# Moving the second modulation of an adaLN block from the rows to the turned expert tiles

## The reference

```python
mod = (silu(c) @ wmod).reshape(2, 6, 1, 128); sa, ca, ga, sb, cb, gb = mod
h = layernorm(x) * (1 + ca) + sa
x = x + ga * recurrence(h)            # block-diagonal gates, then y[t] = a[t]*y[t-1] + b[t]
h = layernorm(x) * (1 + cb) + sb      # the second modulation: by batch, by column
logits = silu(h @ rw1 + rb1) @ rw2 + rb2          # 128 -> 512 -> 8
top 2 of 8, softmax over the two
out = sum_e we * (silu(h @ w1[e] + b1[e]) @ w2[e] + b2[e])
x = x + gb * out
```

## Time and profile before

| | |
|---|---|
| three runs | 289.06, 290.06, 291.38 us; median 290.06 |
| the profiled execution | 288.09 us, its span 286.2 us, so 1.9 us lie outside the span |
| busy in the span | PE 248.1, DVE 188.4, POOL 171.6, ACT 166.5 us |
| mean granted TensorE clock | 0.956 |

### The profile page before, as it was taken

One profiled execution on the slowest core, in us unless ns is written; L12 is line 12 of the kernel. 1 busy time (PEld: TensorE's weight loads), 2 busy tenths in 40 slices (PEclk: granted clock), 3 DMA queues, 4 the chain that ended last, 5 costly groups with the idle time before them and its releaser, 6 DMA issues.

```text
span 286.2 us, 4950 instructions
## 1 busy us (share of the span) xinstructions
PE 248.1 (87%) x1179; PEld 178.0 (62%) x1179; DVE 188.4 (66%) x750; ACT 166.5 (58%) x322; POOL 171.6 (60%) x192
## 2 busy tenths in 40 slices
PE   7767759997599798999999999999999999989910
PEld 6424334444144245687878888888888888868700
DVE  3959999999999987576444444444444446866533
ACT  4189979999785355545555555555555556445300
POOL 4996211267777757777777777644554445645650
PEclk9997979999779799999999999999999999999995
DMA  7993011121131226413533333222217822280505
GB/s 222 308 333 117 19 40 38 37 75 50 55 121 48 89 82 157 114 47 115 149 84 85 111 101 109 57 75 75 74 46 214 221 72 74 84 256 4 161 0 147
DMA packets 45365, 30.51 MB, mean 107 GB/s; under 512 B 5085, under 2 KB 41999, under 8 KB 45342
## 3 DMA queue, kind: packets, MB, share of 16 engines
q1 hardware_dynamic: 40432, 21.75, 27.9%
q0 software_dynamic: 4544, 8.47, 9.0%
q10 hardware_dynamic: 366, 0.04, 0.1%
HBM read 16.39 MB, written 12.67 MB: 102 GB/s over the span
## 4 chain that ended last, share of the span: by engine, by line
PE 40%; POOL 27%; issue 14%; DVE 12%; DMA 4%; POOLq 1%; DVEq 0%; SPq 0%; ACT 0%
POOL sorted_rows L550 21%; PE bank L1218 18%; PE bank L1205 18%; POOL shared L514 3%; PE bank L1226 3%; PE bank L1194 2%; DVE st L698 2%; DMA expert_out<-shared,tx 2%; POOL rs L506 1%; DVE shared L718 1%; POOL expert_out L559 1%; DVE tx L792 1%; DMA xs<-in_L_attn_x_dram 1%; DVE xs L803 1%; DMA tx<-sorted_rows 1%
## 5 line engine op out<-in xcount | busy, mean ns | idle before, releaser
L559 POOL DMA_INDIRECT expert_out<-shared,tx x78 | 80.4, 1031 | 52.9 <-DVE shared L1012 37.4
L657 ACT ACTIVATE hT<-bank,w_t 128x256 f32<-128x256 f32 x156 | 65.4, 470 | 29.3 <-PE bank L1205 28.3
L550 POOL DMA_INDIRECT sorted_rows<-rows,sloti x64 | 63.9, 999 | 27.2 <-issue 18.3
L1205 PE MATMUL bank<-xT,w_t 128*128 128x256 f32 x312 | 74.1, 380 | 0.1
L1218 PE MATMUL bank<-hT,w_t 128*128 128x256 f32 x312 | 74.1, 380 | 0.0
L1205 PEld LDWEIGHTS bank<-xT,w_t 128*128 128x128 f32 x312 | 56.3, 190 | 6.8 <-DVE w_t L995 0.7
L1218 PEld LDWEIGHTS bank<-hT,w_t 128*128 128x128 f32 x312 | 56.2, 190 | 6.2
L666 ACT ACTIVATE yT<-bank,w_t 128x256 f32<-128x256 f32 x39 | 18.4, 473 | 47.6 <-PE bank L1218 47.6
L1134 PE MATMUL bank<-h2T,rw_s 128*128 128x512 f32 x64 | 36.8, 677 | 1.7 <-ACT qv L644 1.4
L986 DVE COPY xT<-bank 128x256 f32<-128x256 f32 x39 | 16.5, 422 | 23.6 <-PE bank L1194 23.6
L1012 DVE TENSOR_TENSOR shared<-bank,tx 128x256 f32<-128x256 f32 x39 | 16.5, 423 | 21.3 <-PE bank L1226 21.2
(11 more groups left out here) (194 smaller groups left out, 328.9 us busy)
## 6 DMA issues: line engine op xcount, KB each, us to landing
tx<-sorted_rows SPq DMA_DIRECT2D x39, 130.0 KB, 2.2
w_s<-in_L_ffn_w_dram SPq DMA_DIRECT2D x16, 256.0 KB, 6.1
xs<-in_L_attn_x_dram SPq DMA_DIRECT2D x8, 256.0 KB, 5.2
rows<-rows SPq DMA_DIRECT2D x8, 256.0 KB, 2.6
av<-expert_out SPq DMA_DIRECT2D x8, 256.0 KB, 3.7
qv<-expert_out SPq DMA_DIRECT2D x6, 256.0 KB, 5.0
expert_out<-shared,tx POOLq DMA_INDIRECT x78, 2.3
sorted_rows<-padr SPq DMA_DIRECT2D x9, 130.0 KB, 3.0
```

The source lines that it names most:

```text
L550: p.indirect_dma_start(sorted_rows[:, :], bass.IndirectOffsetOnAxis(ap=sloti[:, k, t:t + 1], axis=0), rows[:, t, k, :], None).then_inc(s_d ...
L559: p.indirect_dma_start(expert_out[:, :], bass.IndirectOffsetOnAxis(ap=xr_i[:, s % U, n, D + 1:D + 2], axis=0), yo[:, s % U, n, :], None, b ...
L657: ins = nc.scalar.activation(hsT[:, u % 2, h, :], bank[4 + q][:, (h % 2) * SL:(h % 2 + 1) * SL], ACT.Silu, bias=w1_t[:, u % 2, HID + h:HID ...
L1205: ins = t.matmul(bank[4 + h // 2][:, (h % 2) * SL:(h % 2 + 1) * SL], w1_t[:, u % 2, h * P:(h + 1) * P], xT[:, u % 2, :], start=True, stop= ...
```

## The change

The second modulation leaves the rows. `norm2` now writes the plain layernorm, one pass of four tensor_scalar instructions. The router's copy (`copy`, ACT) applies (1 + cb) and sb as scale and bias of its activation, by batch. The expert tiles apply them in `xT` (DVE), on the turned tile: batch 0's values on all 256 columns, and for tiles 9 and up a second instruction that writes batch 1's values from a split column k on. k is a third row of the table, read into a register (a TENSOR_LOAD) for each tile; sorted rows of batch 0 come before those of batch 1. The first nine tiles need no second instruction. `mod2` and `mods2` make the two columns; `rowsA` now handles one vector instead of three.

Further: the copies `w2` go from DVE to ACT, behind `hid`; the row places become twelve (SLOTS) and the loop begins with tile 12 (FIRST), so tiles 10 and 11 have places of their own; the clamps of groups 0 to 3 go to POOL as one tensor_scalar (min with 1) of 128x512 each, and `mult` of these groups takes 0.25 - 0.25 q in its own scale and bias; DVE instead of POOL normalizes groups 0 to 3 and 7, POOL groups 4 to 6; the 11 matmuls `warm` at the start are gone; `PLAN` is new on all engines; the sums of groups stand in steps 32 to 37 and 40 instead of 31 to 34, 36, 37 and 40.

```diff
     U = 10
-    FIRST = 11
+    FIRST = 12
+    SLOTS = 12
...
-    POOLED = 3
+    CLAMPED = 4
+    POOLED = (4, 5, 6)
...
+            def no_more_than_one(g):
+                pool.wait_ge(s_exp, g + 1)
+                p.tensor_scalar(qv[:, cols(g)], qv[:, cols(g)], 1.0, None, ALU.min).then_inc(s_up, 1)
...
             def multiplier(g):
-                act.wait_ge(s_u, g + 1)
-                nc.scalar.activation(qv[:, cols(g)], qv[:, cols(g)], ACT.Sqrt).then_inc(s_m, 1)
+                if g < CLAMPED:
+                    act.wait_ge(s_up, g + 1)
+                    nc.scalar.activation(qv[:, cols(g)], qv[:, cols(g)], ACT.Sqrt, bias=gac[:, 2, 0:1],
+                                         scale=-0.25).then_inc(s_m, 1)
...
-                nc.scalar.copy(h2T[:, g % 2, :], turn_bank("turn_h", g)[:, :]).then_inc(s_h2T, 1)
+                nc.scalar.activation(h2T[:, g % 2, :], turn_bank("turn_h", g)[:, :], ACT.Identity,
+                                     bias=modc[:, 3, b:b + 1], scale=gac[:, 3, b:b + 1]).then_inc(s_h2T, 1)
...
+            def weights2(s, u):
+                e = act.value_load(tab[0:1, 1, bass.ds(s, 1)], min_val=0, max_val=NE - 1)
+                if not (static(s) and s < 2):
+                    act.wait_ge(s_yT_e, s - 1)
+                nc.scalar.copy(w2_t[:, u % 2, :], w2_s[:, bass.ds(e * W2E, W2E)]).then_inc(s_w2t, 1)
...
             def ln2_norm(g):
-                    ins = v.scalar_tensor_tensor(rows[:, t, 0, 0:D], xs[:, t, :], mv2[:, t, 0:1], cbB[:, b, :],
-                                                 ALU.subtract, ALU.mult)
...
-                    ins = v.scalar_tensor_tensor(rows[:, t, 0, 0:D], rows[:, t, 0, 0:D], rs2[:, t:t + 1],
-                                                 sbB[:, b, :], ALU.mult, ALU.add)
+                    ins = v.tensor_scalar(rows[:, t, 0, 0:D], xs[:, t, :], mv2[:, t, 0:1], rs2[:, t:t + 1],
+                                          ALU.subtract, ALU.mult)
...
             def take_x(s, u):
-                v.tensor_copy(xT[:, u % 2, :], bank[1][:, 0:SL]).then_inc(s_xT, 1)
+                early = static(s) and s < EARLY
+                v.tensor_scalar(xT[:, u % 2, 0:SL], bank[1][:, 0:SL], gac[:, 3, 0:1], modc[:, 3, 0:1],
+                                ALU.mult, ALU.add).then_inc(s_xT if early else s_xa, 1)
+                if not early:
+                    k = dve.value_load(tab[0:1, 2, bass.ds(s, 1)], min_val=0, max_val=SL)
+                    dve.wait_ge(s_xa, s - EARLY + 1)
+                    v.tensor_scalar(xT[:, u % 2, bass.ds(k, SL)], bank[1][:, bass.ds(k, SL)], gac[:, 3, 1:2],
+                                    modc[:, 3, 1:2], ALU.mult, ALU.add).then_inc(s_xT, 1)
```

More of the change, by code:

```diff
@@ L260, in adaln_block @@
             "tensor": """
[L261 to L264, removed]
@@ L282, in adaln_block @@
[L282 to L291 removed]
+                turnc:0 mod:0 turn_x:0 turn_x:1 gates:0 gates:1 turn_x:2 mod2:0 turnb:0 turn_x:3 gates:2 gates:3
@@ new lines, in adaln_block @@
+            "scalar": """
+                csil:0 esp:0 modulate:0 modulate:1 tanh:0 decay:0 tanh:1 decay:1 modulate:2 mult:0 modulate:3 mult:1
+                tanh:2 modulate:4 tanh:3 decay:2 modulate:5 decay:3 tanh:4 mult:2 copy:0 mult:3 decay:4 tanh:5
+                modulate:6 decay:5 silu:0 clamp:4 silu:1 clamp:5 silu:2 copy:1 silu:3 mult:4 lgc:0 mult:5 silu:4
+                silu:5 share:0 copy:2 silu:6 silu:7 copy:3 lgc:1 silu:8 silu:9 tanh:6 modulate:7 silu:10 share:1
+                silu:11 decay:6 lgc:2 clamp:6 mult:6 silu:12 tanh:7 silu:13 copy:4 silu:14 share:2 silu:15 decay:7
+                lgc:3 silu:16 silu:17 copy:5 silu:18 clamp:7 share:3 silu:19 mult:7 lgc:4 silu:20 silu:21 copy:6
+                silu:22 silu:23 silu:24 silu:25 share:4 lgc:5 silu:26 copy:7 silu:27 w2:0 silu:28 share:5 lgc:6
+                silu:29 silu:30 silu:31 w2:1 hid:0 share:6 yb:0 lgc:7 hid:1 w2:2 hid:2 yb:1 share:7 w2:3 hid:3 yb:2
+                hid:4 w2:4 yb:3 hid:5 w2:5 yb:4 hid:6 yb:5 w2:6 hid:7 yb:6 w2:7 hid:8 yb:7 w2:8 hid:9 w2:9 yb:8 hid:10
+                yb:9 w2:10 hid:11 w2:11""",
@@ L298, in adaln_block @@
+                rstd2:0 clamp:2 clamp:3 rstd1:6 norm1:6 rstd2:1 rstd1:7 rstd2:2 rstd2:3 send:0 send:1 send:2 send:3
+                send:4 send:5 send:6 send:7 send:8 send:9 send:10 send:11 send:12 send:13 send:14 send:15 scat:0
+                scat:1 scat:2 scat:3 scat:4 scat:5 scat:6 scat:7 scat:8 scat:9 scat:10 scat:11 scat:12""",
         }
@@ L921, in early_table @@
                 dve.wait_ge(s_cnt, 1)
+                v.tensor_copy(first[:, :], bank[7][:, 0:NE])
                 yield from link(v.tensor_tensor(cmpk[:, :, :, :], bank[7][:, 0:NE].unsqueeze(2).unsqueeze(3)
@@ L1083, in modulation, with modulation2 @@
                 ins.then_inc(s_modc, 1)
+            def modulation2(_):
+                pe.wait_ge(s_modok, 1)
+                for i in range(3, 5):
+                    ins = t.matmul(bank[6][:, i * B:(i + 1) * B], wmod_s[:, i * D:(i + 1) * D], csil[:, :],
+                                   start=True, stop=True)
+                ins.then_inc(s_modc, 1)
             def modulation_rows(_):
-                pe.wait_ge(s_modok, 1)
+                pe.wait_ge(s_modok, 2)
                 pe.wait_ge(s_csb, 1)
```

230 lines of the change are left out of this document (119 added, 111 removed).

## The result

The changed kernel takes 294.79 us (median of 6 runs, 293.02 to 296.72), the kernel before 290.21 (6 runs, 288.67 to 291.44). The ratio is 1.0159, 95% interval 1.0099 to 1.0219. Run again later on another chip it took 294.19 against 290.80 us, ratio 1.0103 (1.0060 to 1.0146). The profiled execution of the change lasted 295.58 us (span 293.8) against 288.09 (span 286.2), so the two traces differ by 7.6 us where the medians differ by 4.6.

The account below looks back on a forecast made before the run. It took POOL's 64 unbroken sends, then PE's pace over the expert tiles, to bound the kernel. Terms -2.0 - 0.7 + 1.7 + 2.4 = +1.4 us gave 289.5 for the profiled execution, 291.5 us for the median; range 286.0 to 296.5.

Parts of the forecast that it names:

- Part 1: Stage up to the first send: less DVE and ACT work moves that send from 58.18 to about 56 us, -2.0 us.
- (b): First stage: POOL's clamps take 3.2 us each, shrinking the first send's gain to 0.4; kernel 293.1 us; chance 0.15.
- the prediction's own slope: First stage: `place:0` ends at about 54.8 us with a clamp of 1.3 us, about 57.4 with one of 3.2.
- tile 0's layer would start near 104 us: Start of the expert tiles: DVE's saved work lets tile 0 start at about 104 instead of 111.5 us.
- Part 2: From the last send to tile 9's layer: earlier start, -0.7 us; PE's lower clock after waiting, +1.7 us.
- a wait of some 5 us: Before tile 9: PE waits some 5 us for its load, then runs some 3.5 us at the lower clock.
- Part 3: Loop: second `xT` write releases the bank 1.89 us after the turn, 0.12 us lost in each of 20 steps, +2.4 us.
- Edits at no cost: `w2` on ACT, the moved sums in steps 32 to 37, the removed `warm` matmuls: 0 each, 1 us bound for the last two.
- (d): Loop: the release comes 0.35 us late in each step, costing 7 us; kernel 296.1 us; chance 0.12.
- (c): Ahead of `place:0`: DVE's two-operand instructions stand still during POOL's clamps, 5.2 us lost; kernel 296.7 us; chance 0.06.
- (a): Front half pays: `place:0` ends near 54.3 us (-3.6), the loop loses nothing; kernel 286.6 us; chance 0.15.
- (e): Loop: no stall there and the rest as forecast; kernel 289.1 us; chance 0.17.

Follow-up runs that it names:

- mended: The changed kernel with clamps of groups 0 to 3 on ACT, split column loaded before the wait, later turns back in their own bank: 285.96 us, ratio 0.9836.
- changed_again: The changed kernel run once more without any edit, on another chip: 294.19 us against 290.80 for the kernel before, ratio 1.0103.
- clamps_act: The changed kernel with the clamps of groups 0 to 3 back on ACT: 338.09 us on a slow chip, ratio 1.0272 to the kernel before.
- kept_busy: `mended` with eleven 128x128 identity products in PE's two idle pieces around the turn of tile 9: 285.24 us, ratio 0.9855 to the kernel before.
- ten_places: `mended` with ten row places instead of twelve, tile 11's step in the loop, sums at the former steps: 287.19 us, ratio 0.9919 to the kernel before.
- old_order: The change's computation in the former order, engines and ten row places, without warming products, with early column load and own bank: 286.78 us, ratio 0.9903.
- old_early: `old_order` with `mods2:0` moved forward, right behind `input:1` on DVE: 284.50 us, ratio 0.9784 to the kernel before.
- one_write: The changed kernel with a single write of the turned tile, batch 1's second write left out: 330.42 us on a slow chip, ratio 0.9982.
- own_bank: The changed kernel with the turns back of tiles 10 and later in PSUM bank 2 instead of 1: ratio 1.0007 to the kernel before.

## Why the prediction was right in sign and short in size

Forecast +1.4 us on the profiled execution, found +7.5; forecast 291.5 us for the median, found 294.8, inside the range. Two of the four terms were wrong, and a third came out on a premise that failed.

**Part 1, the first send: forecast -2.0, found +2.5.** This term failed in sign. The step that failed is the sum, "`place:0` ends at about 54.8 us with a clamp of 1.3 us", far more than the price of a clamp in it. (54.8 and the 1 us added are 55.8, not 55.9; and rival (b) leaves the 1 us out of its 0.4, with it the rival stands at 294.0.) Groups of the changed kernel:

```profile
L528 POOL TENSOR_SCALAR shared<-xs,mv,rs 128x128 f32<-128x128 f32 x12 | 11.0, 928 | 0.3
L534 POOL TENSOR_SCALAR qv<-qv 128x512 f32<-128x512 f32 x4 | 6.5, 1631 | 2.5 <-ACT qv L628 2.5
```

A clamp takes 1.63 us. By the prediction's own slope (2.6 us of `place:0` for 1.9 us of clamp) that is only 0.5 us more, of 4.5 that the term is off. The runs showed 3.7 us for having the clamps on POOL (`mended` against `changed_again`; the bank and the register edits act after the sends), and 2.0 to 2.6 us on the first chip (`clamps_act`). What the slope lacked, as far as the traces show, is PE's clock, which fell in the wait for `norm1:5` (the gate products of group 4 took 3.5 us there against 1.9 in `mended`) and again behind 46 us (1.5 us), and `norm1` itself, 928 ns an instruction against 823 in `mended` and 821 in the earlier trace rows. The clamps push `norm1` to a later time, at which three of its instructions ran beside VectorE's `scan` and took 1.26 to 1.38 us, the others 0.79 to 0.81. Which of these holds the first send, and by how much, no run separates. Without the clamps the first send goes at 57.1 us (56.7 in `kept_busy` and `ten_places`), 1.1 to 1.5 us before that of the kernel before: the new order and the single pass of `norm2` are worth that much, over half of the 2.0.

That tile 0's layer would start near 104 us was wrong too: it started at 111.74. Tile 0's load was issued at 106.02, against 106.08 before, and that these agree is chance: before, it waited for the table `tab`, which DVE wrote at 105.09, long after the first 32 sends had gone out. In the change the table is ready at 99.03, so DVE did save 6.1 us there, about the 6.5 that I had put behind `place:0`; but now the landing of the 32nd send, at 104.58, is the gate (the copy of group 7's rows, ahead of it on SP, was over at 104.49), and it is late with the first send. I had said that of the last send and not seen it for the first half.

**Part 2, the handover: forecast -0.7 and +1.7, found -0.73 and +1.69.** The first holds step by step: the load of tile 9 is issued 3.08 us after the last send starts, lands in 2.24, and two writes and `tx:10` follow. The second is right in size by luck in part. Its premise was a wait of some 5 us, since tile 0 would start near 104, and tile 0 did not: PE idled 1.97 and 1.51 us in two pieces, and lost as much as forecast for one of 5. That idling is the cause `kept_busy` supports, since with the pieces filled the clock stays; how much idling it takes stays open, for `old_order` idled 2.44 us there at no loss and `old_early` 2.18 us with it. `ten_places` shows that the twelve places give 0.9 us there. It was no chance: each of the five traces of the new order without the filling products, outside the first chip of the experiments, has it (5.60, 5.61, 5.61, 5.45 and 5.37 us for `tx:10` to `tx:11`), and `old_early` (5.63) too.

**Part 3, the loop: forecast +2.4, found +5.7.** The mechanism is right (`one_write`, `own_bank`); the step that failed is the size of the release. The release was put at 0.51 + 0.93 + 0.45 = 1.89 us after the turn; it is 0.52 + 1.01 + 0.54 = 2.07. Two operands from memory cost a write 0.12 us over the copy's 0.42, where I allowed 0.06, and they cost it twice, since the gap starts when the first write ends. Over what is free (1.77) that is 0.30 us a step, 0.28 by the steps' length, where 0.12 was forecast; over 20 steps that makes the difference of 3.3 us. The written-out steps before the loop lost nothing, as forecast.

**Edits at no cost.** `w2` on ACT cost nothing in the loop: with it, the steps are 3.90 us. The sums' steps gained 0.7 us, inside the bound of 1. The `warm` products: 0.3 us at the first send on one chip, and nothing measurable in the time.

**The rivals.** (b), POOL's clamps, and (d), the loop, both came true in part, and at once: the loop is between the forecast and (d), which wanted 0.35 us a step. (b) was to decide from 2 us a clamp and did so at 1.63. (c), that POOL and DVE exclude each other for the length of a clamp, did not happen: the one `input` that ran beside a clamp (at 20.69 us) took 0.69 us, as alone, and the clamps took 1.49 to 1.79. There is a stretching. Beside the clamps, four of DVE's norms took 0.52 to 0.71 us, against 0.34 for the others beside them; beside `norm1` on POOL two `input`s took 0.90 and 0.80. The Trainium skill's "SBUF — State Buffer", section "Who interferes with whom", names instructions with two SBUF inputs as those that contend with GpSimd's reads, and `input` and `scan` beside `norm1` bear that out; priced as a full lock of a clamp's length, as I did for that rival, it would be several times too dear for this trace. (a) and (e) fell with the loop.

## What to carry to other kernels

When an instruction is added between a PSUM bank's fill and its release, add up the release to the hundredth, gaps and register loads included, and compare it with the next use of the bank; if it is near, give the next user another bank or take the register load out, before asking whether the rest pays. Moving work to an engine with time to spare costs nothing only while nobody waits for that engine: here 6.5 us of clamps on POOL delayed the first send by 3.7 us on one chip and by 2.0 to 2.6 on another. Ask of each gate (here the 32 and the 64 sends) whether saved work lies ahead of it or behind it.

## What the hardware showed unexpectedly

- VectorE took 543 ns for a multiply and add of 128x256 from PSUM with two operands from memory, 0.12 us more than the copy (0.42 us).
- GpSimd took 1.49 to 1.79 us for a minimum of 128x512 with a constant, and for a `norm1` of 128x128 0.79 to 0.81 us alone and 1.26 to 1.38 beside VectorE's `scan`.
- TensorE's granted clock fell to the lower level after two idle pieces with one turn between them (0.8 to 3.2 us ahead of it, 1.5 to 2.4 behind it), and eleven small products in these pieces kept it at 1.00 (`kept_busy`), though 1.51 us of idling were left. It also fell after a single piece of 2.18 us (`old_early`), and not after one of 2.44 (`old_order`).
- GpSimd's sends need 1.26 us each at their best (0.96 and 0.30 between). From the first to the last it was 83.6 us in the change, 84.5 before and 83.1 in `mended`; 82.0 and 81.6 in `old_order` and `old_early`, which began at 60 us.
